# A graph kernel's layer loop: TensorE's unrolled main loop becomes an engine loop of four units with fixed mark places

## The chip, the cores and the metric

The kernel runs on one core of one Trainium2 chip. The metric is the device time of one execution in microseconds (us): before the change 12940.66 us, the median of three runs (12935.49 to 12972.4).

## The reference, cut to what matters

12500 nodes with 32 features and 200000 edges, sorted by destination. A layer norm and relu, then twelve graph layers (eight "lift", four "proj"), then a second graph stage (a "conv" over the same edges), which the change does not touch. A layer is:

```python
def _max_cut_grad(x, src, dst, edge_weight, num_nodes):
    msg = x[src] * edge_weight[:, None]
    return jax.ops.segment_sum(msg, dst, num_segments=num_nodes)

def lift_step(h, wb):
    W, b = wb
    g = _l2_normalize(_max_cut_grad(h, src, dst, edge_weight, N))
    out = jnp.concatenate([h, g], axis=1) @ W + b
    return (_l2_normalize(out), None)
```

A proj layer leaves the two normalisations out and ends in tanh.

## The kernel before, in words

Nodes stand in 128 lanes (partitions) of 100 blocks, 32 features each. Edges were sorted once, before the layers, into slots: a *unit* is a pair of five source blocks and twenty destination blocks. There are 100 units: 5 chunks (destinations, `CHUNKS`) of 20 steps (sources, `STEPS`). For each unit two matrices of zeros and ones, the marks, lie in DRAM, 320 KB each: the *picks* say which source lane a slot takes, the *places* say to which destination lane it goes. A few edges that did not fit are the *spilled* ones, done after the main loop of a layer.

In each of the 12 layers, each unit goes through these steps:

- SyncE loads the unit's picks and places into one of five places of a ring (`load_marks`, line 649). Both halves of a place wait for the same event: the sums of the unit five earlier are done (`unit_added`).
- TensorE gathers (`gather`, L1927): 60 small products. The stationary operand is 32 columns of `parts`, the features split into three bf16 parts, at an address that depends on the step; the moving operand is the picks.
- ScalarE copies the two result banks to SBUF (L1622).
- TensorE turns them (`turn_slots`, L1942), five fp32 transposes.
- VectorE weighs and splits them in six instructions of 320 elements (`weigh_unit`, L1141, L1147, L1151, twice each).
- TensorE adds (`add_unit`, L1959): 20 products of places and messages into four PSUM banks, `unit_sums`.

TensorE's order for step q is: turn unit q, gather unit q+1, add unit q-1 (`add_chunk`, L1968). After the last unit of a chunk VectorE sums the four banks into `hg` (`join_chunk`, L1158, four reductions), and TensorE clears the banks with four products (`clear_unit_sums`, L1950) in step 1 of the next chunk, between the gather and the first add. VectorE's order around this is: weigh the first unit of the next chunk, then join. The sum of a chunk's last unit is issued before the turn of the next chunk's first unit.

All 100 units are written out one after another in TensorE's program; only the loop over the 12 layers is an engine loop. TensorE waits at the layer's start for `parts_ready`, which VectorE signals when all four chunks of the new features are split (L1205). VectorE, ScalarE and SyncE run loops over chunks with 20 steps written out. GpSimd gathers the spilled rows beside the main loop, one indirect DMA (L771) for each of the first 72 units.

After the main loop come the spilled edges (L1993 to L2004) and the dense part (L2019, L2034), each limited by other waits; then the features go to the DRAM table, ScalarE copies them into `hg` (L1613), and the next layer starts.

## Time and profile before

| what | value |
|---|---|
| median of three runs | 12940.66 us |
| span of the profiled execution, first to last instruction | 11187.8 us |
| median minus span | 1752.9 us |
| TensorE, matmul busy | 7977.6 us, 71% |
| TensorE, weight loads | 5606.9 us, 50% |
| VectorE busy | 9110.1 us, 81% |
| ScalarE busy | 3152.1 us, 28% |
| GpSimd busy | 4719.6 us, 42% |

The profile gives the span of its execution; its own time outside the span was not recorded, so the median of the runs stands beside it. The sorting ends and the marks are made by about 2815 us, the twelve layers lie between about 2815 and 7697 us, the second graph stage behind them. Busy shares are means over these stages; the layers have to be read by themselves.

### The profile page before, as it was taken

The page shows a single profiled execution, that of the slowest core. Times are in us where ns is not written, and L with a number is a line of the kernel's source. Part 1 is how long each engine was busy: PE and PEld are TensorE (multiplying, and loading weights), DVE is VectorE, ACT ScalarE, POOL GpSimd, SP SyncE. Part 2 cuts the span into 40 slices and gives each one's busy share as a digit, 9 for nine tenths or more (in the row PEclk, how much of TensorE's full clock was granted, in tenths as well). Part 3 has the DMA queues.
Part 4 walks back from the last instruction along what each step waited for, and adds up shares of the span by engine and source line. Part 5 has one row for each costly group of instructions (what it writes and reads, how often), then busy time and mean ns, then how long its engine had stood idle before and what let it go on. Part 6 is the DMA issues. An engine that isn't in the chain of part 4 may idle for free.

```text
span 11187.8 us, 339090 instructions
## 1 busy us (share of the span) xinstructions
PE 7977.6 (71%) x127894; PEld 5606.9 (50%) x127895; DVE 9110.1 (81%) x18642; ACT 3152.1 (28%) x7975; POOL 4719.6 (42%) x5783
## 2 busy tenths in 40 slices
PE   2555555400777877877877878786889988888994
PEld 2444444300666766766766767674444444444442
DVE  8777777658877877877877877778999999999995
ACT  0111111048222222222222222222444444444441
POOL 3777777610311311321221221232665656666661
PEclk9999999975988988988988988997665666566555
DMA  4111111147645655744745755662111111111111
GB/s 174 26 26 25 25 25 25 27 168 249 200 150 152 205 152 151 211 151 150 216 150 152 211 168 161 182 186 77 36 36 35 34 36 36 36 35 35 36 34 19
DMA packets 719340, 1175.84 MB, mean 105 GB/s; under 512 B 155346, under 2 KB 350241, under 8 KB 715001
## 3 DMA queue, kind: packets, MB, share of 16 engines
q1 hardware_dynamic: 435480, 1024.95, 28.9%
q0 software_dynamic: 146832, 67.20, 5.1%
q10 hardware_dynamic: 136012, 67.95, 2.4%
q8 instruction: 906, 14.84, 0.6%
q14 instruction: 110, 0.90, 0.0%
HBM read 1019.27 MB, written 140.22 MB: 104 GB/s over the span
## 4 chain that ended last, share of the span: by engine, by line
PE 41%; DVE 18%; issue 16%; ACT 3%; POOL 1%; DVEq 1%; DMA 1%; ACTq 0%; POOLq 0%; SPq 0%
PE psum L1959 10%; PE psum L1927 10%; PE psum L1942 6%; PE psum L2069 6%; PE psum L2050 3%; DVE space L1476 2%; DVE space L1475 2%; DVE space L1442 2%; PE psum L2034 2%; PE psum L2004 2%; DVE space L1480 2%; ACT space L1590 2%; DVE space L1487 1%; PE psum L2019 1%; ACT space L1595 1%
## 5 line engine op out<-in xcount | busy, mean ns | idle before, releaser
L714 POOL TENSOR_TENSOR claim_out<-claim_in 128x1 f32<-128x1 f32 x1199 | 309.9, 258 | 4943.4 <-DMA table<-space 2405.5
L789 POOL DMA_INDIRECT space<-feature_table,space x2000 | 1943.1, 972 | 612.0 <-issue 611.6
L2050 PE MATMUL psum<-w_mix,space 64*128 64x448 f32 x4144 | 1755.8, 942 | 0.0
L1622 ACT ACTIVATE space<-psum 128x375 f32<-128x375 f32 x2400 | 937.9, 435 | 2866.9 <-PE psum L1927 2862.6
L725 POOL DMA_INDIRECT slots<-space x1568 | 1507.0, 961 | 466.1 <-issue 412.8
L1141 DVE TENSOR_TENSOR space<-psum,space 128x320 f32<-128x320 f32 x2400 | 1065.7, 485 | 727.6 <-PE psum L1942 702.8
L1927 PE MATMUL psum<-space 128*32 128x125 fp8e4 x72000 | 1344.0, 223 | 227.5 <-issue 226.1
L1959 PE MATMUL psum<-space 128*128 128x96 bf16 x24000 | 1287.9, 206 | 217.8 <-issue 163.1
L1927 PEld LDWEIGHTS psum<-space 128*32 128x32 bf16 x72000 | 1077.4, 97 | 484.2 <-issue 474.0
L1959 PEld LDWEIGHTS psum<-space 128*128 128x128 fp8e4 x24000 | 1099.4, 96 | 375.6 <-issue 258.4
L1147 DVE TENSOR_TENSOR space<-space 128x320 f32<-128x320 f32 x2400 | 1059.5, 482 | 2.7 <-issue 2.7
L1151 DVE TENSOR_TENSOR space<-space 128x320 f32<-128x320 f32 x2400 | 1061.5, 483 | 0.0
L2069 PEld LDWEIGHTS psum<-space 128*128 128x128 f32 x4000 | 746.2, 287 | 594.8 <-DVE space L1487 577.1
L2069 PE MATMUL psum<-space 128*128 128x32 f32 x4000 | 779.3, 364 | 329.7 <-DVE space L1487 327.3
L771 POOL DMA_INDIRECT space<-table,space x864 | 835.2, 967 | 336.2 <-issue 326.1
L1942 PE MATMUL psum<-identity,space 128*128 128x128 f32 x6000 | 904.4, 282 | 66.7 <-ACT space L1622 42.5
L1438 DVE TENSOR_TENSOR space<-psum,space 128x512 f32<-128x512 f32 x1036 | 707.4, 683 | 243.7 <-PE psum L2050 240.6
L1867 PE MATMUL psum<-space 128*128 128x100 bf16 x1568 | 295.3, 278 | 826.0 <-DVE space L960 690.7
L1699 ACT ACTIVATE space<-space,b_col,w_col 128x256 f32<-128x256 f32 x518 | 309.6, 598 | 1675.3 <-PE psum L2050 1666.5
L1715 ACT ACTIVATE space<-columns,space 128x128 bf16<-128x128 f32 x2072 | 655.2, 387 | 185.3 <-issue 175.6
L1942 PEld LDWEIGHTS psum<-identity,space 128*128 128x128 f32 x6000 | 649.9, 143 | 92.3 <-ACT space L1622 56.8
L2050 PEld LDWEIGHTS psum<-w_mix,space 64*128 64x128 f32 x4144 | 481.8, 284 | 360.4 <-issue 360.4
(275 smaller groups left out, 11948.6 us busy)
## 6 DMA issues: line engine op xcount, KB each, us to landing
space<-marks SPq DMA_DIRECT2D x2400, 320.0 KB
marks<-space SPq DMA_DIRECT2D x100, 640.0 KB, 3.1
space<-distances ACTq DMA_DIRECT2D x200, 320.0 KB
space<-block_ids SPq DMA_DIRECT2D x198, 200.0 KB
slots<-space SPq DMA_DIRECT2D x82, 448.0 KB, 9.1
space<-feature_table,space POOLq DMA_INDIRECT x2072, 2.4
space<-src_rows SPq DMA_DIRECT2D x102, 320.0 KB, 4.0
slots<-space POOLq DMA_INDIRECT x1608, 2.1
```

Of the source, the lines that this page charges most:

```text
L725: g.indirect_dma_start(out=slots, out_offset=bass.IndirectOffsetOnAxis(ap=stage_row[:, s, c:c + 1], axis=0), in_=stage[:, s, c, :], in_off ...
L771: g.indirect_dma_start(out=spill_rows[:, t, :], out_offset=None, in_=table, in_offset=bass.IndirectOffsetOnAxis(ap=spill_rec[:, t, 0:1].bi ...
L789: g.indirect_dma_start(out=gathered_rows[:, half, t, :], out_offset=None, in_=feature_table, in_offset=bass.IndirectOffsetOnAxis(ap=row_in ...
L1141: v.tensor_tensor(row[:, half, :], slots_of_unit[:, half, :], slot_w[:, bass.ds(at * UNIT_TILES + k * HALF_TILES, HALF_TILES)].rearrange(" ...
L1147: v.tensor_tensor(left[:, half, :], row[:, half, :], tops[0][:, half, :], ALU.subtract).then_inc(left_split, 1)
L1151: v.tensor_tensor(least[:, half, :], left[:, half, :], tops[1][:, half, :], ALU.subtract).then_inc(least_split, 1)
L1622: a.activation(to[:, s0:s1, :, :], pair_picked[:, bank, 0:(s1 - s0) * PICK_COLS].rearrange("p (k c r) -> p k c r", k=s1 - s0, r=CAP), ACT.Copy
L1927: last = mm(pair_picked[D * g:D * (g + 1), bank, (s - s0) * PICK_COLS:(s - s0 + 1) * PICK_COLS], parts[:, q * SRC_PER_TILE + s, c, :], cel ...
L1942: last = nc.tensor.transpose(slots_of_unit[:, c * LANE_GROUPS:(c + 1) * LANE_GROUPS, :].rearrange("p t d -> p (t d)"), picked[:, q % 2, c, ...
L1959: last = mm(unit_sums[:, t // SUMS_PER_BANK, to:to + PARTS * D], mark_ring[:, q % RING, 1, t * LANES:(t + 1) * LANES], message_halves[:, q ...
L2050: last = mm(radial[:, 2 * ring + odd, 0:MIX_S + MIX_V], hidden[odd * HIDDEN:(odd + 1) * HIDDEN, slot, upper * LANES:(upper + 1) * LANES], ...
L2069: last = mm(conv_sums[:, tile // SUM_BLOCKS, to:to + D], lane_marks[:, ring, :], edge_messages[:, BUFFER_OF[g] * GROUP + t, :], start=Fals ...
```

## The change

TensorE's main loop becomes three nested engine loops: layer, chunk, and a turn of four units (`PLACES` = 4). Marks of unit n always come to place n mod 4, so that addresses in the body are constants. The stationary operand of the gathers can't be addressed by step any more without registers, so ScalarE copies each unit's 15 source matrices (480 bf16 elements per lane) from `parts` into one of four places `unit_parts`, two units ahead, behind the two result copies. The fifth ring place holds them. Two units before the loop and up to two behind it are written out. SyncE loads the picks of unit n+4 when unit n is gathered, and the places of unit n+4 when unit n is added; in its order each load of places stands behind the load of picks of four units later. A chunk's last add now comes behind the turn of the next chunk's first unit and the gather of its second; the clear comes right behind that add. One product of one column is put ahead of the 20 of each add. TensorE loads the count of turns of a chunk from SBUF (`value_load`), 48 tiny products are put at the program's start, and a wait on `parts_ready` moves from TensorE to ScalarE, which starts its first two copies at a new signal given when the first chunk of features is split.

```diff
--- before.py
+++ after.py
@@ -95,8 +95,13 @@
...
     UNIT_COLS = UNIT_TILES * LANES
-    RING = 5
-    assert STEPS % RING == 0 and UNITS % 2 == 0
+    RING, RING_WORDS = 5, 2 * UNIT_COLS // 4
+    PLACES = 4
+    LAYER_FILL, CONV_FILL = 48, 0
+    assert STEPS % PLACES == 0 and PLACES < RING
+    CHUNK_TURNS = STEPS // PLACES
+    SOURCE_WORDS = SRC_PER_TILE * 3 * D // 2
+    assert PLACES * SOURCE_WORDS <= RING_WORDS
     PICK_BANKS = ((0, 3), (3, 5))
...
@@ -321,6 +327,8 @@
...
         mark_ring = ring_flat.bitcast(FP8).rearrange("p (r k c) -> p r k c", r=RING, k=2)
+        unit_parts = ring_flat[:, PLACES * RING_WORDS:PLACES * (RING_WORDS + SOURCE_WORDS)].bitcast(BF16).rearrange(
+            "p (r s c d) -> p r s c d", r=PLACES, c=PARTS, d=D)
         source_ring = ring_flat[:, 0:UNIT_COLS // 2].bitcast(U8).rearrange("p (s c) -> p s c", s=2)
...
@@ -645,26 +655,37 @@
...
 
+            picks = slice(0, UNIT_COLS // 4)
+            places = slice(UNIT_COLS // 4, 2 * UNIT_COLS // 4)
+
+            def load_picks(at, place):
+                sp.dma_start(ring_words[:, place, picks], marks[bass.ds(at, 1), :, picks].rearrange("a p c -> (a p) c")
+                             ).then_inc(picks_loaded[place], 16)
+
+            def load_places(at, place):
+                sp.dma_start(ring_words[:, place, places], marks[bass.ds(at, 1), :, places].rearrange("a p c -> (a p) c")
+                             ).then_inc(places_loaded[place], 16)
+
             with sp.Fori(0, LAYERS, 1) as layer:
-                def load_marks(j, q):
-                    at = q if isinstance(j, int) else sp.snap(j * STEPS + q, min_val=0, max_val=UNITS - 1)
-                    sp.wait_ge(unit_added, layer * UNITS + j * STEPS + q + 1)
-                    for half, loaded in enumerate((picks_loaded, places_loaded)):
-                        words = slice(half * UNIT_COLS // 4, (half + 1) * UNIT_COLS // 4)
-                        sp.dma_start(ring_words[:, q % RING, words],
-                                     marks[bass.ds(at, 1), :, words].rearrange("a p c -> (a p) c")
-                                     ).then_inc(loaded[q % RING], 16)
-
-                for q in range(RING):
-                    load_marks(0, q)
+                sp.wait_ge(unit_added, layer * UNITS + RING)
+                for q in range(PLACES):
+                    load_picks(q, q)
+                    load_places(q, q)
                 sp.wait_ge(h_ready, layer + 1)
...
                              h.rearrange("p b d -> p (b d)")).then_inc(table_stored, 16)
-                for q in range(RING, STEPS):
-                    load_marks(0, q)
-                with sp.Fori(1, CHUNKS, 1) as j:
-                    for q in range(STEPS):
-                        load_marks(j, q)
+                for q in range(PLACES):
+                    sp.wait_ge(pair_gathered, layer * (2 * UNITS) + 2 * q + 2)
+                    load_picks(q + PLACES, q)
+                with sp.Fori(0, UNITS // PLACES - 2, 1) as i:
+                    for q in range(PLACES):
+                        sp.wait_ge(pair_gathered, layer * (2 * UNITS) + i * (2 * PLACES) + 2 * (q + PLACES) + 2)
+                        load_picks(sp.snap(i * PLACES + q + 2 * PLACES, min_val=0, max_val=UNITS - 1), q)
+                        sp.wait_ge(unit_added, layer * UNITS + i * PLACES + q + RING + 1)
+                        load_places(sp.snap(i * PLACES + q + PLACES, min_val=0, max_val=UNITS - 1), q)
+                for q in range(PLACES):
+                    sp.wait_ge(unit_added, layer * UNITS + UNITS - 2 * PLACES + q + RING + 1)
+                    load_places(UNITS - PLACES + q, q)
 
...
@@ -826,6 +847,8 @@
...
             v.tensor_copy(ones_bf[:, :], ones[:, :]).then_inc(bf_ready, 1)
+            v.memset(chunk_turns[:, 0:CHUNKS - 1], CHUNK_TURNS).then_inc(bf_ready, 1)
+            v.memset(chunk_turns[:, CHUNKS - 1:CHUNKS], CHUNK_TURNS - 1).then_inc(bf_ready, 1)
             v.tensor_scalar(half_of_lane[:, 0:1], own_lane[:, 0:1], float(HALF), None, ALU.is_lt)
...
@@ -1203,6 +1226,8 @@
...
                 last = v.tensor_tensor(parts[:, at, 2, :], work[:, at, :], parts[:, at, 1, :], ALU.subtract)
+                if c == 0:
+                    last.then_inc(parts_started, 1)
                 if c + 1 == DENSE_CHUNKS:
...
@@ -1606,11 +1631,22 @@
...
             a.activation(stat2[:, :], stat2[:, :], ACT.Sqrt).then_inc(deviation_ready, 1)
+            for place in range(MADE_RING):
+                act.wait_ge(marks_stored[place], 16 * (UNITS // MADE_RING))
 
...
                     a.activation(hg[:, :, 0:D], h, ACT.Copy).then_inc(h_copied, 1)
+
+                    def copy_sources(q):
+                        return a.activation(unit_parts[:, q % PLACES, :, :, :],
+                                            parts[:, q * SRC_PER_TILE:(q + 1) * SRC_PER_TILE, :, :], ACT.Copy)
+
+                    act.wait_ge(parts_started, layer + 1)
+                    for q in range(2):
+                        copy_sources(q).then_inc(sources_copied, 1)
+                    act.wait_ge(parts_ready, layer + 1)
                     with act.Fori(0, CHUNKS, 1) as j:
...
@@ -1623,6 +1659,7 @@
...
                                              ).then_inc(pair_copied, 1)
+                            copy_sources((q + 2) % STEPS).then_inc(sources_copied, 1)
 
...
@@ -1822,7 +1859,14 @@
...
 
-            pe.wait_ge(bf_ready, 2)
+            def fill(products):
+                for _ in range(products):
+                    mm(psum[:, 8 * BANK - 1:8 * BANK], zeros_bf[:, 0:LANES], zeros_bf[:, 0:1], start=True, stop=True)
+
+            pe.wait_ge(bf_ready, 4)
+            pe.wait_ge(cleared, 1)
+            fill(LAYER_FILL)
+            pe.wait_ge(bf_ready, 4)
             pe.wait_ge(cleared, 1)
...
@@ -1918,30 +1962,29 @@
...
 
-            def gather(layer, n, q):
-                cells = mark_ring[:, q % RING, 0, :].rearrange("p (c g l) -> p c g l", g=LANE_GROUPS, l=LANES)
+            def await_unit(layer, turn, o):
+                pe.wait_ge(picks_loaded[o % PLACES], 16 * turn + 16 * (o // PLACES) + 16)
+                pe.wait_ge(sources_copied, 2 * layer + PLACES * turn + o + 1)
+
+            def gather(o):
+                place = o % PLACES
+                cells = mark_ring[:, place, 0, :].rearrange("p (c g l) -> p c g l", g=LANE_GROUPS, l=LANES)
                 for bank, (s0, s1) in enumerate(PICK_BANKS):
...
                                 last = mm(pair_picked[D * g:D * (g + 1), bank, (s - s0) * PICK_COLS:(s - s0 + 1) * PICK_COLS],
-                                          parts[:, q * SRC_PER_TILE + s, c, :], cells[:, :, g, CAP * s:CAP * (s + 1)],
+                                          unit_parts[:, place, s, c, :], cells[:, :, g, CAP * s:CAP * (s + 1)],
                                           start=c == 0, stop=c == PARTS - 1)
...
 
-            def loads_of(layer, j, q):
-                return (layer * CHUNKS + j) * (STEPS // RING) + q // RING + 1
-
-            def await_picks(layer, j, q):
-                pe.wait_ge(picks_loaded[q % RING], 16 * loads_of(layer, j, q))
-
-            def turn_slots(n, q):
-                pe.wait_ge(pair_copied, 2 * n + 2)
-                pe.wait_ge(weighed, 2 * n + 2)
+            def turn_slots(turn, o):
+                pe.wait_ge(pair_copied, 2 * PLACES * turn + 2 * o + 2)
+                pe.wait_ge(weighed, 2 * PLACES * turn + 2 * o + 2)
                 for c in range(COLS_OF):
...
                         slots_of_unit[:, c * LANE_GROUPS:(c + 1) * LANE_GROUPS, :].rearrange("p t d -> p (t d)"),
-                        picked[:, q % 2, c, :], identity[:, :])
+                        picked[:, o % 2, c, :], identity[:, :])
                 last.then_inc(slots_turned, 1)
...
@@ -1950,41 +1993,46 @@
...
 
-            def add_unit(layer, j, n, q):
-                pe.wait_ge(bf_ready, 2)
-                pe.wait_ge(places_loaded[q % RING], 16 * loads_of(layer, j, q))
-                pe.wait_ge(least_split, 2 * n + 2)
+            def add_unit(turn, o):
+                pe.wait_ge(places_loaded[o % PLACES], 16 * turn + 16)
+                pe.wait_ge(least_split, 2 * PLACES * turn + 2 * o + 2)
+                mm(unit_sums[:, 0, 0:1], zeros_bf[:, 0:LANES], zeros_bf[:, 0:1], start=False, stop=True,
+                   skip_group_check=True)
                 for t in range(UNIT_TILES):
...
                     last = mm(unit_sums[:, t // SUMS_PER_BANK, to:to + PARTS * D],
-                              mark_ring[:, q % RING, 1, t * LANES:(t + 1) * LANES],
-                              message_halves[:, q % 2, t, :, :, 1].rearrange("p c d -> p (c d)"),
+                              mark_ring[:, o % PLACES, 1, t * LANES:(t + 1) * LANES],
+                              message_halves[:, o % 2, t, :, :, 1].rearrange("p c d -> p (c d)"),
                               start=False, stop=True, skip_group_check=True)
...
 
-            def add_chunk(layer, j, more):
-                first = (layer * CHUNKS + j) * STEPS
-                for q in range(STEPS):
-                    if q + 1 < STEPS or more:
-                        await_picks(layer, j + (q + 1) // STEPS, (q + 1) % STEPS)
-                    turn_slots(first + q, q)
-                    if q + 1 < STEPS:
-                        gather(layer, first + q + 1, q + 1)
-                    elif more:
-                        gather(layer, first + STEPS, 0)
-                    if q == 1:
-                        clear_unit_sums(layer * CHUNKS + j)
-                    if q:
-                        add_unit(layer, j, first + q - 1, q - 1)
-                add_unit(layer, j, first + STEPS - 1, STEPS - 1)
-
             with pe.Fori(0, LAYERS, 1) as layer:
-                pe.wait_ge(parts_ready, layer + 1)
-                await_picks(layer, 0, 0)
+                layer_turns = UNITS // PLACES
+                await_unit(layer, layer * layer_turns, 0)
                 mm(slots_of_unit[:, 0, :], zeros_bf[:, 0:LANES], zeros_bf[:, 0:D], start=True, stop=True)
-                gather(layer, layer * UNITS, 0)
-                for j in range(CHUNKS):
-                    add_chunk(layer, j, j + 1 < CHUNKS)
+                gather(0)
+                await_unit(layer, layer * layer_turns, 1)
+                turn_slots(layer * layer_turns, 0)
+                gather(1)
+                with pe.Fori(0, CHUNKS, 1) as j:
+                    clear_unit_sums(layer * CHUNKS + j)
+                    turns = pe.value_load(chunk_turns[0:1, bass.ds(j, 1)], min_val=CHUNK_TURNS - 1, max_val=CHUNK_TURNS)
+                    with pe.Fori(0, turns, 1) as m:
+                        turn = layer * layer_turns + j * CHUNK_TURNS + m
+                        for o in range(PLACES):
+                            await_unit(layer, turn, o + 2)
+                            turn_slots(turn, o + 1)
+                            gather(o + 2)
+                            add_unit(turn, o)
+                last_turn = layer * layer_turns + layer_turns - 1
+                for o in range(PLACES):
+                    if o + 2 < PLACES:
+                        await_unit(layer, last_turn, o + 2)
+                    if o + 1 < PLACES:
+                        turn_slots(last_turn, o + 1)
+                    if o + 2 < PLACES:
+                        gather(o + 2)
+                    add_unit(last_turn, o)
 
...
```

## Rows read from the trace of the kernel before

**Rows 1.** The page: span, and the instruction queue (packets, MB, share).
```profile
span 11187.8 us, 339090 instructions
...
q8 instruction: 906, 14.84, 0.6%
```

**Rows 2.** Stretches: length; PE, PEld, DVE, ACT, POOL busy (count); clock, DMA share, GB/s.
```profile
3234.00:3550.00 316.00, 268.40 (x8427) 230.32 (x8426) 255.77 (x611) 77.35 (x198) 89.05 (x144) 0.98 0.70 208
sum 3752.00, PE 3205.60 PEld 2750.12 DVE 3068.26 ACT 927.40 POOL 1075.11; mean PE 267.13 PEld 229.18 DVE 255.69 ACT 77.28 POOL 89.59
```

**Rows 3.** Waits over the span: who for whom, total us, times, longest.
```profile
DVE space L1141 <- PE psum L1942: 702.8, 584, 5.5
...
PE psum L1927 <- issue: 226.1, 219, 2.9
PE psum L1959 <- issue: 163.1, 159, 3.4
```

**Rows 4.** Timeline, first layer: start, us, engine and line [idle before].
```profile
3106.59 0.89 DVE L1141 TENSOR_TENSOR space<-psum,space 128x320 f32<-128x320 f32 x2
...
3107.36 1.04 PE L1959 MATMUL psum<-space 128*128 128x96 bf16 x20
...
3108.24 0.73 PE L1942 MATMUL psum<-identity,space 128*128 128x128 f32 x5
...
3109.09 0.89 DVE L1141 TENSOR_TENSOR space<-psum,space 128x320 f32<-128x320 f32 x2
...
3110.75 0.47 PE L1927 MATMUL psum<-space 128*32 128x125 fp8e4 x20 [1.10 <-issue]
```

**Rows 5.** Instruction queue in the second main loop, and behind it (3550 to 3650).
```profile
q8 instruction: 66, 1.08, 1.5%
...
q8 instruction: 9, 0.15, 0.7%
```

**Rows 6.** TensorE's groups in the conv loop, 8000 to 10300 us.
```profile
L2050 PE MATMUL psum<-w_mix,space 64*128 64x448 f32 x2884 | 1218.3, 939 | 0.0
...
L2047 PE MATMUL psum<-space,ones_bf 3*128 3x448 bf16 x1442 | 371.2, 512 | 5.0 <-DVE space L1442 5.0
```

**Rows 7.** Timeline of a chunk's end, first layer.
```profile
3009.99 0.89 DVE L1141 TENSOR_TENSOR space<-psum,space 128x320 f32<-128x320 f32 x2 [2.00 <-PE psum L1942]
...
3012.41 2.34 DVE L1158 TENSOR_REDUCE space<-psum 128x480 f32 x4
...
3014.67 0.88 DVE L1141 TENSOR_TENSOR space<-psum,space 128x320 f32<-128x320 f32 x2
...
3014.80 0.98 PE L1950 MATMUL psum<-zeros 128*128 128x480 bf16 x4 [1.56 <-DVE space L1158]
```

**Rows 8.** Sequencer instructions of single lines: ns min/median/max.
```profile
L2084 PEldq COMPARE_BRANCH  x40: 76/208/237, 7810.0 to 10293.5; - x40
...
L1989 PEldq TENSOR_LOAD <-spill_turns x12: 308/313/318, 3136.2 to 7627.9; - x12
...
L1956 PEldq EVENT_SEMAPHORE  x1200: 51/51/51, 2821.9 to 7627.6; - x172
...
L654 SPq DMA_DIRECT2D space<-marks x2400: 327/333/1826, 2781.5 to 7617.0; - x185
```

**Rows 9.** Stretches before and after a stop of TensorE, columns as in rows 2.
```profile
2996.00:3000.40 4.40, 1.97 (x79) 1.68 (x79) 2.49 (x6) 0.88 (x2) 0.96 (x1) 1.00 0.67 206
3000.40:3003.80 3.40, 3.40 (x76) 2.88 (x73) 1.64 (x5) 0.65 (x2) 1.16 (x2) 0.50 0.41 109
```

**Rows 10.** Timeline at the start of the second layer.
```profile
3224.70 2.98 ACT L1613 ACTIVATE space<-space 128x3328 f32<-128x3328 f32 x1 [2.12 <-DVE space L1232]
...
3230.24 0.20 PE L1984 MATMUL psum<-zeros 128*128 128x32 bf16 x1 [14.51 <-DVE space L1205]
...
3234.09 0.89 DVE L1141 TENSOR_TENSOR space<-psum,space 128x320 f32<-128x320 f32 x2 [4.00 <-PE psum L1942]
```

**Rows 11.** Groups: ScalarE's copy of up to 512 elements.
```profile
L1645 ACT ACTIVATE space<-space 128x512 f32<-128x512 f32 (+1 forms) x56 | 33.2, 594 | 16.9 <-DVE space L1240 16.7
```

**Rows 12.** The page: a DMA issue with KB and time to landing.
```profile
marks<-space SPq DMA_DIRECT2D x100, 640.0 KB, 3.1
```

More of the change, by code:

```diff
@@ L239, in build_gnn @@
         count_i = sb("count_i", [1, 1], I32)
+        chunk_turns = sb("chunk_turns", [1, CHUNKS], I32)
         half_offsets = sb("half_offsets", [1, LANES * HALF_COLS], I32)
@@ L486, in build_gnn @@
         parts_ready = sem("parts_ready")
-        picks_loaded = [sem(f"picks_loaded{i}") for i in range(RING)]
-        places_loaded = [sem(f"places_loaded{i}") for i in range(RING)]
+        parts_started = sem("parts_started")
+        sources_copied = sem("sources_copied")
+        picks_loaded = [sem(f"picks_loaded{i}") for i in range(PLACES)]
+        places_loaded = [sem(f"places_loaded{i}") for i in range(PLACES)]
         pair_gathered = sem("pair_gathered")
@@ L2038, in _ @@
                 pe.wait_ge(biased, layer * OUTS + OUTS)
+            fill(CONV_FILL)
             pe.wait_ge(weights_spread, 16 * 3)
```

## The prediction

> **What bounds the kernel now.** I read the busy time by stretch first, then the waits, then the timeline of single units. In the twelve main loops of the layers (3752 us of the span of 11187.8) VectorE is busy 255.69 us of 312.7 on average and TensorE 267.13 [rows 1, 2]. VectorE's idle time there is one wait: L1141, the first instruction of a unit, waits 702.8 us in all for TensorE's turn L1942 [rows 3]. That is nearly all that this change can win. In an undisturbed unit nothing waits: L1141 starts at 3106.59 and again at 3109.09, 2.50 us a unit, with VectorE and TensorE both full [rows 4]. A layer has 99 steps from its first weighing to its last. Four of them hold a join and take 3014.67-3009.99 = 4.68 us [rows 7]. The others so take (312-4x4.68)/95 = 3.09 us instead of 2.50.
>
> What makes 2.50 into 3.09? TensorE stops for "issue" in the middle of a group, after 40 of 60 products for 1.10 us [rows 4], in all 226.1+163.1 = 389 us before L1927 and L1959, at 378 places [rows 3]. In one main loop the instruction queue moved 66 packets of 1.08 MB, 16 KB each, for 8427 products and 8426 weight loads: 255 instructions a packet, so 64 bytes each [rows 2, 5]. TensorE's code is written out and fetched anew in every layer: 12x(66+9) = 900 of the program's 906 packets [rows 1, 5]. The stops are late fetches, 389/12 = 32 us a layer. The rest of the 95x0.59 = 56 us: 2.0 us at each chunk's end, where the turn of the next unit stands behind the last add [rows 7], 8 us; five clears of about 0.9 us [rows 7], 4 us; some stretches at half clock (1.2 instead of 2.4 GHz) after a long stop [rows 9], 4 us; about 8 us I can't name.
>
> **The change, part by part.** All terms are us per layer and counted against the profiled execution; its span is 1752.9 us under the median, and I carry that part over unchanged and subtract the gain from the median.
>
> *The loop.* A turn has 4x86 = 344 products, with the weight loads 688 instructions and some 40 for waits and branches, about 730x64 B = 46 KB, three or four packets. If it stays in the engine's buffer, fetches and stops go. What shows this? The conv loop's turn on TensorE is five groups of 40 products (8 of L2047, 16 of L2050, 16 of L2069, by the counts 2884 and 1442 and the code), 400 instructions or 26 KB, over 2300 us; yet the whole program outside the layers fetched 6 packets [rows 1, 5, 6]. So at least two packets stay; three or four no row shows. I take it that they stay. Then 95 steps at 2.50 = 237.5.
>
> The Trainium skill ("Runtime: NRT & Kernel Launch", Instruction fetch mechanics) gives TensorE 128 KiB, eight such blocks, but says in the same place that the buffer is only two cache lines and that a taken branch to a target outside this window stalls for a fetch. The conv loop agrees with either; by the first the loop runs free, by the second rival A comes true.
>
> *The product ahead of each add.* 20 products with their loads take 3108.24-3107.36 = 0.88 us, 0.044 each [rows 4]; TensorE has no slack: 95x0.044 = 4.2. Nothing, if VectorE alone bounds, is the lower end.
>
> *Waits.* Today a unit has one register instruction and one of 51 ns such as L1956 [rows 8]; then six waits against registers, and the one for `sources_copied` is new. Behind them stand all products of TensorE, and VectorE behind its turn. Three or four more at 0.05 are 0.15 to 0.2, mostly while the queue still holds products; I take 0.05 a unit, 95x0.05 = 4.8 (0 to 19).
>
> *The back edge.* 24 a layer, 208 ns [rows 8] and register work, at most about 0.4, behind 20 queued products: I take 0.3 at the 20 inside a chunk, 6.0 (0 to 8).
>
> *The chunk's end.* The turn of the next chunk's first unit now comes ahead of the last add: the 2.0 us are gone (inside the 237.5). But the clear now stands ahead of the second unit's turn, and VectorE waits for both: join 2.26, clear 0.9, turn until the weighing 3109.09-3108.24 = 0.85 [rows 4, 7]. The count's load (0.31 and its checks) and the inner loop's start go on beside the clear and past it by about 0.65. So 2.5+2.26+0.9+0.85+0.65 = 7.2 instead of 4.68; four are 28.7 (26 to 30). TensorE also stands idle about 2.9 us there. In such a stretch, 1.97 us busy of 4.40, the engine was followed by 3.4 us at a clock of 0.50 [rows 9], which costs 1.7; I take one time in two, 4x0.85 = 3.4 (0 to 6.8).
>
> *Code around the loop.* Two units ahead and four behind are still fetched: some four late packets of 0.8, 3.0. The first clear and load: 1.0.
>
> *Marks.* Picks get more time than today. Places get less: their load stands on SyncE behind the load of picks four units later, so it starts when this unit is gathered, two units or 5.0 us ahead of its add. Two issues of 0.333 [rows 8] and a landing: the only row for 640 KB, stores, has 3.1 us [rows 12]. That makes 3.9, inside 5.0; but DMA's share, 0.70 at 3.15 us a unit [rows 2], goes to 0.88 at 2.5, and SyncE's issue has a maximum of 1.826. I take 2.0 (0 to 19).
>
> *ScalarE's copy.* 480 elements, about 0.57 us by 594 ns for 512 [rows 11]; ScalarE is busy 77.28 of 312.7 [rows 2], the copy stands behind the unit's own copies and is due a unit later: nothing. Without that cover it would be 0.57 a unit.
>
> *The layer's start.* TensorE began at 3230.24, after the last split; ScalarE's copy of the features ended at 3227.68, with the first source copy it is about 3228.4 [rows 10]. 1.8 earlier, in the eight layers with such a start; in proj layers the two are level. About -1 a layer. The 48 products at the start run while TensorE waits for sorted data: nothing.
>
> Sum: 237.5+4.2+4.8+6.0+28.7+3.4+3.0+1.0+2.0 = 290.6, against 312.0; with the start 22.4 a layer, 12x22.4 = 269 us. 12940.66-269 = 12670.
>
> With all lower ends: 237.5+0+0+0+26+0+0+1+0 = 264.5, 582 less, 12360. With all upper ends 237.5+4.2+19+8+30+6.8+4+1+19 = 329.5: 200 more, 13140, which takes every mishap at once.
>
> **Rivals.** A, slower: the body does not stay. Each turn fetches its three or four packets again and the branch's target is not fetched ahead. 24 turns stop for about 2.4 us (single stops go to 2.9 and 3.4 [rows 3]), 58 us; the other two thirds of the packets cost as now, 21 us. 290.6+79-312 = 58 more a layer: 12940+690 = 13630. It decides from the point where the buffer holds fewer packets than the turn spans. For it: no row shows more than 26 KB kept. Against: the packets' size alone makes two lines a small buffer for an engine that needs a packet each 1.4 units, and the conv loop can span three.
>
> B, late marks: places land 5.8 instead of 3.9 us after the gather, and a unit can't be shorter than half of that, 2.9. My ordinary step is (237.5+4.2+4.8+6.0+2.0)/95 = 2.68; 95x0.22 = 21 more a layer, 250 in all: about 12920, hardly a gain. For it: DMA's share. Against: TensorE's turn shows no wait on marks worth a row today.
>
> C, extras hide: VectorE's 2.50 stays the bound, the product, the waits and the branch lie under its work. 15 less a layer, 180 in all: 12490.
>
> **How the numbers follow.** My sum and its neighbours (12500 to 12830) 0.60; C or better 0.17; B and no effect 0.13; A 0.10. Likeliest 12670; range 12400 to 12900, for 8 in 10: C and part of B inside, A outside. A change of 0.3%, 39 us, is what a measurement can tell from none. Faster by more: 0.85; within: 0.04; slower: 0.11.
>
> **What would show it.** The instruction queue: 15 packets a layer or so, 150 to 250 in all, instead of 906 (A: as many as now or more). L1927's and L1959's "issue" waits under 100 us together. VectorE's step 2.55 to 2.7 inside chunks, a small extra each fourth unit; 7 to 8 at a join, 2.5 before it. L1141's wait for L1942 near 430 us instead of 702.8. ScalarE 680 us busier. A wait of L1959 for marks of over 0.05 a unit would show B. I am wrong if the packets stay at 900, or if the steps inside chunks stay above 2.9.

## The result, and the profile after

Twenty executions of each kernel, on one chip: 12948.33 us before, 12992.29 after, ratio 1.0033 with an interval of 1.0024 to 1.0041. The change made the kernel 0.33% (44 us) slower, a small loss, but the interval leaves out 1; I had forecast 12670 us, 269 less, and gave "slower" 0.11.

The page of the changed kernel, its waits over the span, its second main loop and the sum over all twelve (columns as in [rows 2]), and the layers' part of the span from the first weighing to the last:

```profile
span 12981.3 us, 347519 instructions
...
q8 instruction: 166, 2.72, 0.1%
```

```profile
DVE space L1164 <- PE psum L1985: 1047.8, 948, 6.8
...
PE psum L1976 <- issue: 399.3, 809, 2.4
```

```profile
3744.80:4087.30 342.50, 294.14 (x8505) 238.96 (x8497) 256.04 (x611) 123.39 (x297) 83.80 (x145) 0.97 0.64 188
...
sum 4109.20, PE 3524.85 PEld 2868.38 DVE 3071.96 ACT 1482.43 POOL 1005.07; mean PE 293.74 PEld 239.03 DVE 256.00 ACT 123.54 POOL 83.76
```

```profile
3306.00:8487.00 5181.00, 4183.37 (x109866) 3472.05 (x109869) 3817.44 (x8401) 1732.10 (x4096) 1013.17 (x1748) 0.88 0.53 159
```

In the changed kernel L1164, L1181, L1976, L1985, L1993, L2003 and L792 are the old L1141, L1158, L1927, L1942, L1950, L1959 and L771; L1999 is the new one-column product ahead of each add. Two things don't fit each other. The code fetches went, 166 packets for 906 [rows 1, 5]. Yet a main loop takes 342.4 us, not 312 [rows 2], the layers 5181 instead of 4806, and VectorE waits 1047.8 us for TensorE's turn, more than the 702.8 of [rows 3]. I call it a *stop* when TensorE stands still in the middle of a group and the trace shows nothing that it waits for ("issue"). The timeline of two units, one in the middle of the second chunk and one near the layer's end (start, us, what; in brackets the idle time before), shows why:

```profile
3402.89 1.17 PE L1976 MATMUL psum<-space 128*32 128x125 fp8e4 x50
3403.20 0.96 POOL L792 DMA_INDIRECT space<-table,space  x1 [0.45 <-issue]
3403.22 0.89 DVE L1164 TENSOR_TENSOR space<-psum,space 128x320 f32<-128x320 f32 x2 [1.00 <-PE psum L1985]
...
3404.55 0.36 PE L1976 MATMUL psum<-space 128*32 128x125 fp8e4 x10 [0.49 <-issue]
...
3406.73 0.89 DVE L1164 TENSOR_TENSOR space<-psum,space 128x320 f32<-128x320 f32 x2 [1.02 <-PE psum L1985]
...
3600.68 1.04 PE L1976 MATMUL psum<-space 128*32 128x125 fp8e4 x60
3600.88 0.89 DVE L1164 TENSOR_TENSOR space<-psum,space 128x320 f32<-128x320 f32 x2
...
3603.41 0.89 DVE L1164 TENSOR_TENSOR space<-psum,space 128x320 f32<-128x320 f32 x2
```

Where GpSimd issues an indirect gather (L792, 72 a layer, one a unit, for the spilled rows), TensorE's group of 60 products takes 2.02 us (3402.89 to 3404.91) instead of 1.04, and the unit 3.51 instead of 2.53. The stop ends 1.35 us after the gather's start, in unit after unit. Of the 0.98 us, 0.49 stands in the trace as idle for "issue"; the rest lies in the products on both sides of that gap, which run slower than undisturbed ones (50 in 1.17 us and 10 in 0.36). Behind the last gather of a layer most steps are 2.53 and those with a turn's branch 2.73; the forecast had 2.68 on average.

In the trace that the forecast was read from, gathers start at the same place of a unit, and of the 72 in its second main loop 63 have no stop within 1.6 us of their start, 44 none within 3 us. So either the loop brought the stops, or that trace was of other conditions than the timed runs. Its span of 11187.8 us beside runs of 12940 spoke for the second.

### The profile page after: what moved, and what is told of

Read it like the earlier page. It is cut to its first block, busy times and chain, and to the rows that moved or that the text cites. A ratio compares the mean times of both kernels' runs of the same rounds, so it can differ in the third digit from the quotient of the medians.

```text
span 12981.3 us, 347519 instructions
## 1 busy us (share of the span) xinstructions
PE 8628.6 (66%) x129130; PEld 5886.1 (45%) x129143; DVE 9149.5 (70%) x18644; ACT 3712.2 (29%) x9199; POOL 4631.2 (36%) x5783
## 4 chain that ended last, share of the span: by engine, by line
PE 40%; issue 16%; DVE 14%; another core or an unknown queue 5%; ACT 3%; POOL 1%; DVEq 1%; DMA 0%; ACTq 0%; POOLq 0%; SPq 0%
PE psum L1976 11%; PE psum L2003 7%; PE psum L1985 5%; PE psum L2099 5%; PE psum L2118 4%; DVE space L1467 2%; DVE space L1501 2%; PE psum L2082 2%; PE psum L2052 1%; ACT space L1615 1%; PE psum L2096 1%; DVE space L1500 1%; PE psum L2067 1%; PE psum L1999 1%
## 5 line engine op out<-in xcount | busy, mean ns | idle before, releaser
L735 POOL TENSOR_TENSOR claim_out<-claim_in 128x1 f32<-128x1 f32 x1199 | 235.5, 196 | 6757.9 <-DMA table<-space 2343.7
L2099 PE MATMUL psum<-w_mix,space 64*128 64x448 f32 x4144 | 1954.0, 989 | 35.1 <-issue 34.6
L1976 PE MATMUL psum<-space 128*32 128x125 fp8e4 x72000 | 1621.4, 225 | 424.8 <-issue 399.3
L1164 DVE TENSOR_TENSOR space<-psum,space 128x320 f32<-128x320 f32 x2400 | 1066.7, 486 | 1059.7 <-PE psum L1985 1047.8
L1976 PEld LDWEIGHTS psum<-space 128*32 128x32 bf16 x72000 | 1173.9, 98 | 868.1 <-issue 856.7
L2003 PE MATMUL psum<-space 128*128 128x96 bf16 x24000 | 1247.8, 205 | 1.4 <-issue 1.4
L2118 PEld LDWEIGHTS psum<-space 128*128 128x128 f32 x4000 | 813.3, 310 | 784.4 <-DVE space L1512 481.8
L2118 PE MATMUL psum<-space 128*128 128x32 f32 x4000 | 846.5, 384 | 479.2 <-DVE space L1512 340.2
L2003 PEld LDWEIGHTS psum<-space 128*128 128x128 fp8e4 x24000 | 1099.8, 96 | 2.2 <-issue 1.9
L792 POOL DMA_INDIRECT space<-table,space x864 | 835.0, 966 | 403.4 <-issue 377.5
L1985 PE MATMUL psum<-identity,space 128*128 128x128 f32 x6000 | 904.4, 283 | 41.3 <-ACT space L1658 20.0
L2096 PE MATMUL psum<-space,ones_bf 3*128 3x448 bf16 x2072 | 555.5, 533 | 526.1 <-DVE space L1467 251.8
L1597 ACT ACTIVATE space<-psum 100x400 bf16<-100x400 f32 x392 | 197.6, 504 | 2343.3 <-remote 1590.4
L1911 PEld LDWEIGHTS psum<-space 128*128 128x128 bf16 x1568 | 198.6, 134 | 1401.6 <-DVE space L983 1183.8
```

The lines of the kernel that those rows point to most:

```text
L792: g.indirect_dma_start(out=spill_rows[:, t, :], out_offset=None, in_=table, in_offset=bass.IndirectOffsetOnAxis(ap=spill_rec[:, t, 0:1].bi ...
L1164: v.tensor_tensor(row[:, half, :], slots_of_unit[:, half, :], slot_w[:, bass.ds(at * UNIT_TILES + k * HALF_TILES, HALF_TILES)].rearrange(" ...
L1976: last = mm(pair_picked[D * g:D * (g + 1), bank, (s - s0) * PICK_COLS:(s - s0 + 1) * PICK_COLS], unit_parts[:, place, s, c, :], cells[:, : ...
L1985: last = nc.tensor.transpose(slots_of_unit[:, c * LANE_GROUPS:(c + 1) * LANE_GROUPS, :].rearrange("p t d -> p (t d)"), picked[:, o % 2, c, ...
L2003: last = mm(unit_sums[:, t // SUMS_PER_BANK, to:to + PARTS * D], mark_ring[:, o % PLACES, 1, t * LANES:(t + 1) * LANES], message_halves[:, ...
L2099: last = mm(radial[:, 2 * ring + odd, 0:MIX_S + MIX_V], hidden[odd * HIDDEN:(odd + 1) * HIDDEN, slot, upper * LANES:(upper + 1) * LANES], ...
```

## The experiments

**Before once more (e0).** No edit.

> The kernel before, unchanged, profiled a second time. What it tells apart: the profiled execution of before has a span of 11187.8 us, 1753 us under its runs; that of the changed kernel has 12981.3 us, equal to its runs. In the changed kernel's main loops each of GpSimd's indirect gathers (72 a layer) is followed 0.85 us after its start by a stop of TensorE, and the units with one take 3.50 us, those without 2.53; the first profile of before shows no such stop (44 of 72 gathers have none behind them). Theory S (the first profile caught an execution that is not like the timed ones): this one has a span of 12900 to 13000 us, a stop of TensorE about 1 us long after each of GpSimd's gathers, main loops of about 345 us instead of 312, first layer starting near 3300 instead of 2818, and a conv stage of some 4360 us. Theory L (the stops come from the engine loop of the change): the second profile is like the first, span near 11190, no stop after a gather, and the loss is the change's own.

12822.93 us, and 12858.96 us for a second execution of the same kernel beside it. Its page, twelve main loops and waits:

```profile
span 12821.3 us, 339090 instructions
...
q8 instruction: 906, 14.84, 0.5%
```

```profile
sum 4028.70, PE 3442.90 PEld 2807.72 DVE 3065.36 ACT 915.38 POOL 1009.52; mean PE 286.91 PEld 233.98 DVE 255.45 ACT 76.28 POOL 84.13
```

```profile
DVE space L1141 <- PE psum L1942: 1002.0, 988, 5.5
...
PE psum L1927 <- issue: 445.2, 909, 1.9
...
PE psum L1959 <- issue: 34.4, 39, 1.6
```

Theory S holds: a span of 12821.3 us, main loops of 335.7 us (I had expected 12900 to 13000, and about 345), and a unit of its timeline is that of the changed kernel:

```profile
3778.47 1.14 PE L1927 MATMUL psum<-space 128*32 128x125 fp8e4 x48
3778.78 0.96 POOL L771 DMA_INDIRECT space<-table,space  x1 [0.45 <-issue]
...
3780.07 0.38 PE L1927 MATMUL psum<-space 128*32 128x125 fp8e4 x12 [0.46 <-issue]
```

The stop is the old kernel's too. And the late fetches, which the change was to remove, are mostly gone without it: L1959, which no gather's stop touches, waits 34.4 us for issue instead of 163.1 [rows 3], though all 906 packets are still fetched. At 3.45 us a unit most packets seem to come in time; what L1927 waits for late packets can't be told apart there from the gathers' stops.

**Plain copies instead of gathers (e1, e2, e8, e9, e10).** In the layers each indirect gather became a copy of fixed rows on the same queue, so the spilled rows are wrong ones:

```
-                        g.indirect_dma_start(out=spill_rows[:, t, :], out_offset=None, in_=table, ...
+                        g.dma_start(spill_rows[:, t, :], table[0:LANES, :]).then_inc(spill_gathered[k // 3], 16)
```

> The kernel before, with each of GpSimd's 72 indirect gathers a layer replaced by a plain copy of 128 rows of the table on the same queue (the spilled rows are so not the right ones). Theory I (TensorE's stop belongs to the indirect gather, and it hides the late code fetches that the first profile showed): the stops behind L771's place go, the main loop falls from 335.7 to about 312 us with the late fetches back (steps of 2.5 with stops of 0.5 to 2 us in 30 places a layer); about 290 us less, ratio to before 0.977. Theory Q (any transfer that GpSimd issues stops TensorE): steps stay at 3.44, ratio 0.998 to 1.002.

> The changed kernel with the same plain copies in place of the indirect gathers. By theory I the forecast's loop shows itself: steps of 2.53, and 2.73 at each turn's branch, joins near 8.0, main loop 277 us (forecast 290.6 for such conditions) instead of 342.4; 65 us a layer, 780 in all, ratio to before 0.943, and 400 us under the previous kernel with plain copies. Theory Q: steps stay at 3.50, ratio to before 1.00. A third theory (the forecast's terms are wrong beside the stops too): steps above 2.75 although the stops are gone.

Beside these two the unchanged kernel before took 11185.64 us, as the first trace had it. So the same kernel has two times, and the executions beside each other on one chip all have the same one. I know of no chip that was used on two occasions, so whether it is the chip or the occasion stays open; I write of two kinds of chips all the same. On this kind gathers don't stop TensorE, so these two could not tell I from Q. Plain copies gave the old kernel 0.990 of before (0.9882 to 0.9918) (main loop 302 us: the gathers cost it 10 us a layer without stops too), and the changed one 0.9695 (0.9679 to 0.9711), with a main loop of 281.7 us. Between these two, on one chip, the change is seen without gathers: 906 packets become 166, and the "issue" waits of the gather and the add fall from 183.5 and 131.5 us to 6.7 and 0.6. No run kept the code written out and took the rest of the change, so the packets' part of the 20 us a layer is not measured by itself. Both kernels ran once more beside e7 on another such chip, with 0.990 and 0.9688:

> The kernel before with plain copies in place of GpSimd's indirect gathers in the layers (the spilled rows are not the right ones). Where before takes some 12850 us, theory I (the indirect gather alone stops TensorE): main loop near the 301.9 us that it has on the other chip, 400 us less, ratio 0.969. Theory Q (any transfer issued by GpSimd does): main loop stays at 336, ratio 1.00.

> The changed kernel with the same plain copies. Theory I where before takes some 12850 us: main loop near 282 us, 58 us a layer less than the changed kernel's 339.8, ratio to before 0.95: there too the change is then a gain of 1.5 to 2%. Theory Q: 1.003.

Then the changed one on a chip where before takes 12848.86:

> The changed kernel with plain copies in place of the indirect gathers (the spilled rows are not the right ones), for a chip where before takes some 12850 us; so far it ran where before takes 11190 (main loop 281.7). Theory I (the indirect gather alone stops TensorE): main loop near 282 us instead of 339.8, ratio to before 0.95. Theory Q (any transfer issued by GpSimd does): steps of 3.45, ratio 1.003.

Ratio 0.9472 (0.9448 to 0.9496). The first line is its twelve main loops, the second those of the same kernel on the other kind of chip:

```profile
sum 3375.00, PE 3195.50 PEld 2769.80 DVE 3061.22 ACT 1482.19 POOL 713.54; mean PE 266.29 PEld 230.82 DVE 255.10 ACT 123.52 POOL 59.46
```

```profile
sum 3380.50, PE 3190.24 PEld 2765.98 DVE 3063.84 ACT 1484.42 POOL 715.19; mean PE 265.85 PEld 230.50 DVE 255.32 ACT 123.70 POOL 59.60
```

281.2 us a loop on the one, 281.7 on the other. Theory I: of the two it is the indirect gather that stops TensorE, a plain copy from the same queue doesn't, and without gathers the two kinds of chips don't differ in this loop. The old kernel with plain copies was not run on a chip of this kind.

**The changed kernel beside before, on both kinds of chips (e5, e7).** No edit.

> The changed kernel, unchanged, timed again beside the one before. The first profile of before was of a chip where GpSimd's gathers don't stop TensorE; the timed runs of step one were on one where they do (before: 12948 us there, 11186 us on the chip of the last four kernels). Expected: where before takes some 11190 us, main loops of 282 us by the plain-copy kernel (281.7) plus little, so (312-284) x 12 = 340 us less, 10850, ratio 0.97, a forecast of -269 us (0.976) that was right in kind and low in size. Where before takes some 12900 us: ratio 1.003 again. Rival (the change loses on any chip, and the kernels of the last call won by their own edits): ratio 1.00 or more at 11190.

> The changed kernel, unchanged, beside the one before and the two with plain copies, on one chip. On a chip where before takes some 11190 us: main loop 284 us, 10850 us in all, ratio 0.97 (the ratio with four one-column products was 0.982 there, with the written-out turns 0.966). Where it takes some 12850: ratio 1.003.

| unchanged kernels | before | after | ratio |
|---|---|---|---|
| gathers stop TensorE (e5) | 12835.01 | 12883.13 | 1.0034 (1.0023 to 1.0046) |
| they don't (e7) | 11195.61 | 10940.77 | 0.9772 (0.9759 to 0.9786) |

On the second kind the change takes 255 us off, where I had forecast 269. The page of e7, its main loops and waits:

```profile
span 10947.3 us, 347531 instructions
...
q8 instruction: 167, 2.74, 0.1%
```

```profile
sum 3480.80, PE 3205.49 PEld 2760.11 DVE 3065.71 ACT 1484.79 POOL 1091.32; mean PE 267.12 PEld 230.01 DVE 255.48 ACT 123.73 POOL 90.94
```

```profile
DVE space L1164 <- PE psum L1985: 405.9, 499, 6.7
...
PE psum L1999 <- DMA space<-marks: 94.6, 215, 2.0
...
PE psum L1976 <- issue: 7.3, 5, 2.3
```

and a unit with a gather and no stop:

```profile
3236.39 1.03 PE L1976 MATMUL psum<-space 128*32 128x125 fp8e4 x60
3236.70 0.96 POOL L792 DMA_INDIRECT space<-table,space  x1 [0.36 <-issue]
```

**The first turn of each chunk written out (e3, e6).** The clear goes back to where it was, between the gather and the add:

```
...
+                    for o in range(PLACES):
+                        await_unit(layer, turn, o + 2)
+                        turn_slots(turn, o + 1)
+                        gather(o + 2)
+                        if o == 0:
+                            clear_unit_sums(layer * CHUNKS + j)
+                        add_unit(turn, o)
...
```

with the inner loop one turn shorter.

> The changed kernel with the first turn of each chunk written out ahead of the loop, and the clear in it between the gather and the add, where it stood before. By my reading a join costs 11.3 us over two steps in the changed kernel (5.0 less in the one before it 3.3, 8.04 in its own) and 9.2 before, because clear, turn count and turn stand behind the join while TensorE's clock is at 0.50. Expected: the two steps at 9.2, main loop 342.4 - 4 x 2.1 = 334, 100 us less in all, ratio to before 0.996. If the written-out turns are fetched late: packets of the instruction queue up from 166 to about 400 and steps behind a join of 4 us, ratio 1.000. If the loss isn't at the joins: 1.003 as the changed kernel.

> The kernel with the first turn of each chunk written out (e3) again, beside the changed kernel on the same chip. Where before takes some 12900 us: 4 x 2.1 us less a layer than the changed kernel, 100 in all, ratio to before 0.996. Where it takes some 11190: 0.9656 as measured, and the changed kernel's ratio 0.97 tells what the joins are worth there: (11.3 - 9.2) x 48 = 100 us less a later step 3.4 instead of 2.6 in the written-out turns, 60 in all.

It is the fastest kernel of all that gathers the right rows: 0.9656 (0.9639 to 0.9672) where gathers don't stop TensorE, 0.9892 (0.9876 to 0.9907) where they do. There it is 179 us under the changed kernel on the same chip (12704.48 and 12883.13), more than the 100 that I expected. The changed kernel's join, from the trace of the result, and behind it that of the written-out turn, from e6 (each from the sums' reduction on):

```profile
3377.76 2.35 DVE L1181 TENSOR_REDUCE space<-psum 128x480 f32 x4 [0.34 <-PE psum L2003]
...
3380.17 1.78 PE L1993 MATMUL psum<-zeros 128*128 128x480 bf16 x4 [2.58 <-DVE space L1181]
...
3381.75 1.30 PE L1985 MATMUL psum<-identity,space 128*128 128x128 f32 x5
...
3383.32 0.89 DVE L1164 TENSOR_TENSOR space<-psum,space 128x320 f32<-128x320 f32 x2 [3.21 <-PE psum L1985]
```

```profile
3431.18 2.35 DVE L1181 TENSOR_REDUCE space<-psum 128x480 f32 x4 [0.33 <-PE psum L2003]
3431.27 0.74 PE L1985 MATMUL psum<-identity,space 128*128 128x128 f32 x5 [0.26 <-ACT space L1643]
...
3433.45 0.88 DVE L1164 TENSOR_TENSOR space<-psum,space 128x320 f32<-128x320 f32 x2
3433.59 0.98 PE L1993 MATMUL psum<-zeros 128*128 128x480 bf16 x4
```

In the first, TensorE stands for 2.58 us and is then granted half its clock (0.50, which is 1.2 GHz, from 3380.17 to 3383.05): the clear takes 1.78 instead of 0.98, the turn 1.30 instead of 0.74. Of the 48 joins of that trace 22 have a clear of over 1.5 us and 40 a turn of over 1.0. VectorE waits 3.21 us. In the second VectorE waits for nothing; a join of e6 takes 4.89 us on average, the shortest 4.67. A join and the step before it take 11.3 us in e5 and 8.1 in e6 (means of L1164's starts): 3.1 less, not 2.1, since I had set the written-out pair at the old kernel's 9.2, of which 4.5 is the step before, and that step stays at 3.2 here.

The written-out kernel's instruction queue has 198 packets. The code of its chunk is eight units, 8x172 products and weight loads of 64 B each, 88 KB; it is run five times a layer.

**Four one-column products instead of one (e4).**

> The changed kernel with four one-column products ahead of each add instead of one. If TensorE sets the pace of every unit, three more cost 3 x 0.044 = 0.13 us a unit, 99 x 12 x 0.13 = 157 us, ratio to before 1.0155, and the one of the change is worth 52 us. If they lie beside the stop or VectorE's work, the ratio stays at 1.003, and the product costs nothing.

Ratio 0.9821 (0.9803 to 0.9839), where one product has 0.9772 on another chip of this kind: about 55 us for three, not 157. Main loop 294.8 us (290.1 with one); behind the last gather a step grows by 0.09, 0.03 a product, before it by 0.03 in all. By a third of that, the one product of the change would be worth some 18 us, not 50: an estimate, since to leave it out was not tried.

**Gathers at the joins (e11).** The written-out kernel, with three gathers instead of one behind the last unit of the first three chunks (`paced` counts 0, 1, 2, ... and holds 20, 40 and 60 three times):

```
-                        pool.wait_ge(unit_added, units + RING + t)
+                        pool.wait_ge(unit_added, units + RING + paced[t])
```

> The kernel with the first turn of each chunk written out (e3, e6), and the gathers paced so that three instead of one go out at each of the first three joins, when TensorE waits for VectorE's sums. If a stop costs nothing where TensorE would wait anyway, six stops of 0.95 a layer vanish in part: up to 5.7 us a layer, 68 in all, under e6 (ratio to before 0.9892) on a chip where gathers stop TensorE: 0.984. If every gather costs its 0.95 wherever it is put: 0.989. Where gathers don't stop it: 0.966 as e3.

A miss: 0.9929 (0.9909 to 0.9950), worse than e6. In its timeline a single group of 60 products (L1978 in this kernel) is stopped time and again:

```profile
3363.74 0.25 PE L1978 MATMUL psum<-space 128*32 128x125 fp8e4 x2 [0.39 <-issue]
...
3364.46 0.28 PE L1978 MATMUL psum<-space 128*32 128x125 fp8e4 x5 [0.48 <-issue]
...
3365.21 0.26 PE L1978 MATMUL psum<-space 128*32 128x125 fp8e4 x3 [0.47 <-issue]
3365.94 0.26 PE L1978 MATMUL psum<-space 128*32 128x125 fp8e4 x3 [0.46 <-issue]
3366.65 0.25 PE L1978 MATMUL psum<-space 128*32 128x125 fp8e4 x2 [0.45 <-issue]
```

The step behind such a join went from 2.9 (e6) to 6.3 or more for two gathers more, 1.7 each. So close gathers cost more than spread ones, and the join gave them no cover: with the clear where e6 has it, TensorE goes on while VectorE sums (busy 1.97 of 2.40 us there in e6, from 3431.20).

## Why the prediction was wrong

By its own steps, with the main loop cut in the same way for each kernel (means from the starts of L1141 and L1164; us per layer; each column sets one execution on one chip beside one on another of the same kind):

| | stops: before (e0), after (e5) | no stops: before (first trace), after (e7) |
|---|---|---|
| 61 ordinary steps, units 2 to 71 | 3.455, 3.468: +0.8 | 3.035, 2.712: -19.7 |
| 24 ordinary steps behind them | 2.895, 2.626: -6.5 | 2.994, 2.628: -8.8 |
| 4 joins of three steps | 12.20, 14.65: +9.8 | 12.16, 13.72: +6.2 |
| first two steps | -0.1 | +0.4 |
| main loop | +4.0 | -21.9 (forecast -21.4) |

- *The step that failed* is the frame, not a term: "its span is 1752.9 us under the median, and I carry that part over unchanged". That part was not time outside the span, either: in each recorded run the device time is only 1.6 or 1.7 us longer than the span. By e0 (span 12821.3) the difference is 462 us ahead of the layers (3280 and 2818 us to L1141's first start), 298 in them (5104 and 4806; 285 of it in the main loops, 335.7 and 312.0 us) and 874 behind them (4437 and 3563); in the layers it lies on the very engine and the very steps whose gain was counted. A stop of some 0.95 us a gather sets the unit at 3.45 before the change and 3.47 after it, and at that pace the late fetches have next to no price: of the 56 us a layer above 2.50 that I wanted to win, 6.5 were won in the last 24 steps and 1.3 in the step before each join, and each join took 3.4 more.
- *The code stays in the buffer*: right, 166 packets, I said 150 to 250. The "issue" waits that I wanted under 100 us are 9 in e7; in the result's trace they are 404, the gathers' stops. Rival A is out: the back edge costs 0.20 us (2.73 and 2.53). The Trainium skill ("Runtime: NRT & Kernel Launch", Instruction fetch mechanics) says both 128 KiB and "only 2 cache lines" with a stall at a branch beyond them. The 88 KB that e6 runs through five times a layer with 198 packets in all agree with the first alone.
- *Main loop without stops*: 290.1 us, forecast 290.6; VectorE's wait 405.9 us, forecast 430. Partly by luck: product, waits and back edge were priced at 4.2+4.8+6.0 = 15 and are 2.53 for 2.50 and 0.20 at each fourth, 7; late marks at 2.0 and are 94.6/12 = 7.9. That looks like a part of rival B, but with plain copies, at a still shorter unit, the same wait is 4.3 us in the whole span (e2): the marks are late beside the indirect gathers, not by the pace alone. The first two steps and those behind a join (6.71 and 3.19) are 4.5 us a layer over 2.50 a step, where I had 4.0 for code around the loop. The joins were priced at 7.2 and 0.85 for the clock, 8.0, and take 7.8.
- *The chunk's end* is the term that makes a loss of it under stops. The join's price was right, 7.2+0.85 = 8.0 us, measured 8.04 under stops (e5) and 7.83 without (e7). What was to pay for it, 2.0 us less in the step before, came only without stops (4.54 to 2.69); under them that step goes from 4.51 to 3.23, since its own gather's stop stays. With the step behind, 0.3 us longer, that is 9.8 us a layer instead of 6.2.
- *ScalarE's copy*: nothing, as forecast; 0.60 us each, and ScalarE is busy 123.5 us of a main loop of 342.
- *The layer's start*: next to nothing instead of 1 us a layer. From a loop's last weighing to the next loop's first it is 100.9 us in e0 and 100.5 in e5 behind a lift layer, 89.4 and 90.5 behind a proj layer (one odd gap of 78.4 left out).
- *Outside the layers*: e5 and e0 have 3280 us both ahead of the layers, and 4431 and 4437 behind the last weighing. So the loss lies in the main loops: 12x4.0 = 48 us by these two traces, measured 44 (the result) and 48 (e5). The kernel before differs by more than that from chip to chip (12835 and 12948 us): that there is a loss is shown by the ratios on one chip, and the table only says where it lies.

So the forecast named what the change removes and adds, and was near in size, for one kind of chip, in part because errors cancelled; the runs that it was for were on the other. What stays open is what differs between the chips.

## What to carry to other kernels

A profiled execution 13% shorter than the timed runs of the same kernel is a measurement of something else: find where the difference lies, stage by stage, before a stall of that trace gets a price, for in the timed runs another stall may lie over it and hide it. Where the gap can't be placed, "the stall is hidden in the timed runs" is a rival of its own. And a loop that saves code also moves what stood at a boundary: keep a clear or a turn that was hidden where it was, even if one turn must be written out.

## What the runs showed of the hardware

The kernel before was timed on six occasions. On four of them it takes 12823 to 12948 us, and there all but some 1% of GpSimd's indirect gathers in the main loops stop TensorE, as the traces of the result, e0, e5 and e11 have it: with gathers a unit apart, the group of 60 products takes 0.93 to 0.97 us longer, and the stop ends some 1.3 us after the gather's start. On two (11186 and 11196 us) they don't (e7). The same kernel takes 15% longer on the first kind. Less than a fifth of that lies in the layers (298 of 1634 us). Ahead of them ScalarE and VectorE wait there for signals that the profile can't place ("remote"), where on the other kind they have waits for GpSimd's scatters. For e0, up to 3280 us, and for the first trace, up to 2818:

```profile
ACT space L1572 <- remote: 1545.3, 187, 15.0
...
DVE space L984 <- remote: 591.5, 170, 4.2
```

```profile
ACT space L1576 <- DMA slots<-space: 973.2, 193, 6.0
...
DVE space L982 <- DMA slots<-space: 321.8, 191, 2.6
```

Behind the layers there are such waits too (in e0 1057.4 us for ScalarE's L1699 and 625.7 for VectorE's L1438). GpSimd issues indirect transfers in both parts, 1568 scatters (L725) and 2000 gathers (L789); whether they are the cause there too was not tried. With plain copies in the layers alone, both parts stay as long (3281 and 4455 us in e10).

A plain copy from GpSimd's queue stops TensorE on neither kind (e2, e10). An indirect gather has a price on the kind without stops too: the old kernel gains 120 us (e1) when plain copies stand in their place.
